# One-hots of four tiles made by two 512-wide VectorE instructions instead of four 128-wide ones, in a two-layer graph network

## The reference, cut to what matters

```python
# layer 0
m    = relu(concat(h[src], edge_attr) @ W_msg.T + b_msg)
m    = relu(m @ W_msg2.T + b_msg2)
mean = segment_sum(m, dst) / maximum(count(dst), 1)
x    = x + concat(h, mean) @ W_apply.T + b_apply
# layer 1, on h = relu(layernorm(x))
alpha = softmax of edge_weight over the edges of each destination
agg   = normalise(segment_sum(alpha * h[src], dst))
comb  = normalise(0.5 * (h @ W_self + b_self + agg @ W_nb + b_nb))
x     = x + layernorm(comb) * gamma + beta
```

## Time and profile before

| what | us |
|---|---|
| median of three runs | 8538.44 |
| the profiled execution | 8539.41 |
| its span, first to last instruction | 8537.0 |
| POOL busy | 6174.3 (72%) |
| PE busy | 5259.4 (62%) |
| VectorE busy | 3575.8 (42%) |
| ScalarE busy | 1110.0 (13%) |

### The profile page before, as it was taken

How to read it: one execution, slowest core, us unless ns; L and a number is a source line. 1 busy time by engine, 2 the same in 40 slices (tenths; PEclk the granted TensorE clock), 3 DMA queues, 4 the chain that set the end, 5 groups by cost and what they waited for, 6 DMA issues and landing times.

```text
span 8537.0 us, 114672 instructions
## 1 busy us (share of the span) xinstructions
PE 5259.4 (62%) x26549; PEld 4057.1 (48%) x26549; DVE 3575.8 (42%) x13889; ACT 1110.0 (13%) x1838; POOL 6174.3 (72%) x6510
## 2 busy tenths in 40 slices
PE   4887888888878888887844444444444444444444
PEld 3555655566556665665634334333333333333333
DVE  6344444333443443443454343333333333333336
ACT  2222222222222222222210000000000000000001
POOL 2777777777777777777657777777777777777773
PEclk9988989898898989888865555555555555555555
DMA  5322222222222222233332222111111111111112
GB/s 159 96 79 77 79 75 80 78 79 79 78 78 80 79 79 80 79 87 104 84 95 66 66 65 64 54 53 53 53 53 53 53 53 53 53 53 53 53 53 71
DMA packets 393173, 613.42 MB, mean 72 GB/s; under 512 B 171379, under 2 KB 248927, under 8 KB 392223
## 3 DMA queue, kind: packets, MB, share of 16 engines
q0 software_dynamic: 206336, 422.99, 18.3%
q1 hardware_dynamic: 186784, 189.85, 8.0%
HBM read 576.45 MB, written 35.92 MB: 72 GB/s over the span
## 4 chain that ended last, share of the span: by engine, by line
POOL 61%; issue 23%; PE 8%; DMA 4%; DVE 3%; POOLq 1%; SPq 1%; DVEq 0%; ACT 0%; ACTq 0%
POOL rows_ring L449 61%; PE bank L907 3%; DMA rows_ring<-p_table,idx 2%; PE bank L969 2%; DMA idx<-in_src_ring 1%; PE bank L966 1%; PE bank L904 1%; PE bank L1031 1%; POOLq L443 0%; DVE xq L629 0%; DVE acc L629 0%; POOLq L445 0%; DVE acc L614 0%; DVE stat L597 0%; DVE acc L717 0%
## 5 line engine op out<-in xcount | busy, mean ns | idle before, releaser
L449 POOL DMA_INDIRECT rows_ring<-p_table,idx x3224 | 3070.8, 952 | 1149.0 <-issue 1094.3
L780 DVE TENSOR_TENSOR acc<-acc,bank 128x128 f32 x6448 | 1829.3, 284 | 4826.0 <-PE bank L907 4813.9
L449 POOL DMA_INDIRECT rows_ring<-h_table,idx x3224 | 3050.6, 946 | 1025.7 <-issue 982.2
L907 PE MATMUL bank<-onehot,rows_ring 128*128 128x128 f32 x6448 | 1646.5, 436 | 2322.5 <-DMA rows_ring<-h_table,idx 2322.1
L907 PEld LDWEIGHTS bank<-onehot,rows_ring 128*128 128x128 f32 x6448 | 1415.5, 323 | 2553.4 <-issue 2363.9
L783 DVE TENSOR_SCALAR onehot<-iota,dloc,coef 128x128 f32<-128x128 f32 x6448 | 2340.8, 368 | 20.7 <-ACT coef L503 18.7
L907 PEld LDWEIGHTS bank<-wmat,work 128*128 128x128 f32 x7248 | 1104.0, 219 | 48.9 <-DVE acc L848 9.4
L907 PE MATMUL bank<-wmat,work 128*128 128x128 f32 x7248 | 1100.9, 303 | 11.6 <-DVE acc L848 10.0
L969 PE MATMUL bank<-work,we_sb 64*128 64x512 f32 x1612 | 987.4, 695 | 0.0
L907 PE MATMUL bank<-onehot,work 128*128 128x128 f32 x6448 | 945.3, 295 | 3.0 <-DVE onehot L783 2.9
L966 PE MATMUL bank<-ident,rows_ring 128*128 128x128 f32 x3224 | 546.6, 295 | 628.8 <-DMA rows_ring<-p_table,idx 624.0
(11 more groups left out here) (118 smaller groups left out, 837.9 us busy)
## 6 DMA issues: line engine op xcount, KB each, us to landing
work<-in_edge_t SPq DMA_DIRECT2D x403, 256.0 KB
rows_ring<-p_table,idx POOLq DMA_INDIRECT x3224
rows_ring<-h_table,idx POOLq DMA_INDIRECT x3224, 2.5
idx<-in_src_ring SPq DMA_DIRECT2D x404, 8.0 KB, 1.6
ht_rows<-rows_ring SPq DMA_DIRECT2D x25, 256.0 KB, 2.4
p_table<-rows_ring SPq DMA_DIRECT2D x25, 256.0 KB, 2.5
work<-ht_rows SPq DMA_DIRECT2D x25, 256.0 KB, 2.6
h_table<-work SPq DMA_DIRECT2D x25, 256.0 KB, 2.3
```

Source lines behind the costliest of these rows:

```text
L449: pool.indirect_dma_start(out=rows_ring[:, 16 * h + G * k + j, :], out_offset=None, in_=table[:, :], in_offset=bass.IndirectOffsetOnAxis(a ...
L780: dve.tensor_tensor(win, win, ps_agg[k % 2][:, j * P:(j + 1) * P], ALU.add).then_inc(added, 1)
L907: ins = pe.matmul(tiles(dst)[t], left[t], right[t] if isinstance(right, list) else right, start=bias is None and n == 0, stop=n == len(pai ...
```

## The change

The four `tensor_scalar` instructions of a group are replaced by two `tensor_tensor` instructions over all four tiles: first a comparison of `iota`, repeated four times, with `dloc` broadcast along each tile's 128 columns, and then, in place, a multiplication by `coef`, broadcast in the same way. The comparison stands ahead of the four adds and the multiplication behind them. A new semaphore `hot_compared` orders the second behind the first, and an increment of a counter stands between the wait and the multiplication.

```diff
-            def sums_and_onehots(i, k, lag_sum, lag_hot, in_psum, added, hot):
+            def sums_and_onehots(layer, i, k, lag_sum, lag_hot, in_psum, added, hot):
 
                 adds, hots = live(i, k, lag_sum), live(i, k, lag_hot)
                 gs, gh = 8 * i + k - lag_sum, 8 * i + k - lag_hot
                 if adds:
                     at = bases(gs)
                     dve.wait_ge(in_psum, gs + 1)
-                for j in range(G):
-                    if adds:
-                        if later(gs * G + j):
-                            dve.wait_ge(added, gs * G + j)
-                        win = acc[:, ds(at[j], P)]
-                        dve.tensor_tensor(win, win, ps_agg[k % 2][:, j * P:(j + 1) * P], ALU.add).then_inc(added, 1)
-                    if hots:
-                        t = gh * G + j
-                        ins = dve.tensor_scalar(onehot[:, k % 2, j * P:(j + 1) * P], iota[:, :], dloc[:, ds(t, 1)], coef[:, ds(t, 1)],
-                                                ALU.is_equal, ALU.mult)
                 if hots:
-                    ins.then_inc(hot, 1)
+                    hot4 = four(onehot[:, k % 2, :])
+                    dloc4, coef4 = (arr[:, ds(gh * G, G)].unsqueeze(2).to_broadcast([P, G, P]) for arr in (dloc, coef))
+                    dve.tensor_tensor(hot4, iota[:, :].unsqueeze(1).to_broadcast([P, G, P]), dloc4, ALU.is_equal).then_inc(S["hot_compared"], 1)
+                for j in range(G) if adds else ():
+                    if later(gs * G + j):
+                        dve.wait_ge(added, gs * G + j)
+                    win = acc[:, ds(at[j], P)]
+                    dve.tensor_tensor(win, win, ps_agg[k % 2][:, j * P:(j + 1) * P], ALU.add).then_inc(added, 1)
+                if hots:
+                    dve.wait_ge(S["hot_compared"], layer * NG + gh + 1)
+                    dve.sem_inc(S["vector_turns"], 1)
+                    dve.tensor_tensor(hot4, hot4, coef4, ALU.mult).then_inc(hot, 1)
```

More of the change, by code:

```diff
@@ L166, in gnn @@
             scalars_staged scalars_turned coef_filled sums_zeroed0 dloc_ready x_reloaded
-            counts_made m1t_in_psum m1t_ready m2_in_psum m2_ready onehot0_ready sums0_in_psum sums0_added
+            counts_made m1t_in_psum m1t_ready m2_in_psum m2_ready hot_compared onehot0_ready sums0_in_psum sums0_added
             x1_sums_copied x1_in_psum x1_added var1_ready root1_ready normed1_ready h2_ready sums_zeroed1
@@ L774, in sums_and_onehots @@
                     dve.wait_ge(in_psum, gs + 1)
-                for j in range(G):
-                    if adds:
-                        if later(gs * G + j):
-                            dve.wait_ge(added, gs * G + j)
-                        win = acc[:, ds(at[j], P)]
-                        dve.tensor_tensor(win, win, ps_agg[k % 2][:, j * P:(j + 1) * P], ALU.add).then_inc(added, 1)
-                    if hots:
-                        t = gh * G + j
-                        ins = dve.tensor_scalar(onehot[:, k % 2, j * P:(j + 1) * P], iota[:, :], dloc[:, ds(t, 1)], coef[:, ds(t, 1)],
-                                                ALU.is_equal, ALU.mult)
-                if hots:
-                    ins.then_inc(hot, 1)
+                if hots:
+                    hot4 = four(onehot[:, k % 2, :])
[10 more added lines that the diff above has]
+                    dve.tensor_tensor(hot4, hot4, coef4, ALU.mult).then_inc(hot, 1)
             def layer0(i):
                 for k in range(8):
-                    sums_and_onehots(i, k, 2, 0, S["sums0_in_psum"], S["sums0_added"], S["onehot0_ready"])
+                    sums_and_onehots(0, i, k, 2, 0, S["sums0_in_psum"], S["sums0_added"], S["onehot0_ready"])
             dve.wait_ge(S["coef_filled"], FILLS)
@@ L821, in layer1 @@
                 for k in range(8):
-                    sums_and_onehots(i, k, 2, 0, S["sums1_in_psum"], S["sums1_added"], S["onehot1_ready"])
+                    sums_and_onehots(1, i, k, 2, 0, S["sums1_in_psum"], S["sums1_added"], S["onehot1_ready"])
             dve.wait_ge(S["coef_filled"], 2 * FILLS)
```

## The result

The changed kernel takes 8972.24 us (median of four runs, 8970.26 to 8985.37) against 8538.97 us of the kernel before (8536.38 to 8539.82): a ratio of 1.0511, 95% interval 1.0498 to 1.0525. It is slower by 433 us; the forecast was 9023 us.

A forecast was written before the change was run, and what follows sets the result against it. The prediction took POOL issuing gathers back to back as the bound. To 8539.4 us it added 339 for layer 1 and 161 for layer 0, less 15 for removed one-hots: 9023 us against the median, range 8740 to 9208.

The forecast's parts named there:

- What bounds the kernel: POOL issuing 6,448 gathers back to back, 1.25 us apart: 8060 us, nearly the whole 8537 us span.
- VectorE: Per group, two 0.69 us instructions replace four 0.34 us one-hots: busy time unchanged, longer chain hidden in slack, costing nothing.
- S: Moment TensorE releases VectorE for a group; comparison forecast from it to 0.69 us later, multiplication from about 2.07 us later.
- The mark: 0.12 us after a gather's start; a VectorE instruction with two SBUF inputs running then holds the gather to its end.
- rival B: Faster: two inputs, one broadcast, do not stop POOL's gathers, so only 15 us are won: 8523 us; chance 0.06.
- Layer 1: Comparison hits one gather in each of 806 groups for 0.42 us, multiplication none: 339 us, bounds 81 and 403.
- f: Time from VectorE's release to the start of a gather beside it; in layer 1 claimed locked, 0.19 and 0.06 us shown.
- Rival A2: Layer 1's comparison starts 0.1 later and mostly misses: 0.15 us a group, 121 us instead of 339, 8805 us; chance 0.20.
- A: The forecast case: each comparison in layer 1 hits a gather, 9023 us; chance 0.65.
- Layer 0: Gather starts wander against VectorE's new instructions, so both together delay 0.20 us a group: 161 us, bounds 81 and 282.
- What was removed: Delays of gathers by the old one-hots, which go with the change: 15 us won, bounds 8 and 33.
- The sum: Profiled 8539.4 us plus 339 and 161 minus 15 gives 9024, or 9023 against the median.

The follow-up runs named there:

- e10: Changed kernel with comparison reading the constant row from PSUM and writing to PSUM, multiplication reading that: 8527.08 us in one run, kernel before 8546.43.
- e4: Changed kernel with only the multiplication losing its second SBUF input, the comparison writing to PSUM: 10889.93 us on a slower chip, kernel before 10992.57.
- e5: Changed kernel with only the comparison losing its second SBUF input, constant row read from PSUM: 10988.61 us on a slower chip, kernel before 10992.57.
- c1: The changed kernel unaltered, run again beside the kernel before: 8933.69 us against 8546.43, ratio 1.0456.

## Why the prediction was right, point by point

**What bounds the kernel.** Right, and it still does: the span grew by 431.5 us and the gathers by 432, with "issue" unchanged to 1.1 us.

**VectorE.** The new instructions take 697 and 694 ns where 0.69 was taken from the add of beta. The multiplication starts at S+2.15 in most groups; 2.07 plus up to 0.2 was forecast. The longer chain costs nothing where gathers are the bound: e10 has it whole and takes 8527.08 us.

**The mark.** A gather ends 0.81 to 0.83 us behind the instruction that holds it, as the three rows of before said. That the cause is the second SBUF input, which those rows could only suggest, is shown by e10, with e4 and e5. What the prediction had only as a guess is the other edge, "about 0.05" behind the start of the instruction. For the new instructions it is sharp: gathers that start up to 0.043 us behind one are let through, those that start 0.044 us or more behind it are held. For the old one-hots it is another, about 0.12 us. The clause of the Trainium skill ("SBUF — State Buffer", "Who interferes with whom") by which `tensor_tensor` would leave DMA issue alone does not hold for these indirect gathers; the same section's sentence that two SBUF inputs contend with a GpSimd instruction that reads SBUF fits, if an indirect gather counts as one. No run here separated its reading of the indices from the rest of its work. A broadcast input, rival B's doubt, makes no difference.

**Layer 1, the term that was mis-sized.** Forecast 339 us (0.42 in each of 806 groups), measured 239.6 + 47.3 + 5.1 = 292 us. The step that failed is "the comparison hits one gather in each group" and that f stays locked. f was locked only within the jitter of the landings, and 169 of 803 groups had f below 0.04 (the gather may start up to 0.1 us before the comparison among them). There the comparison lets the gather through (6013.58), and the multiplication catches the second one behind it, for 0.26 us (6016.08). The prediction saw this case and priced it at 0.1 to 0.15; it costs more because the multiplication starts at S+2.15 and not at S+2.07, and because f is about zero or less. That delay falls between the group's last gather and the next ones and so is added to f: 158 of those 169 groups are followed by one with f between 0.2 and 0.5, whose comparison then costs only 0.28 us (6018.83). Rival A2 was thus no alternative to A but a fifth of its groups, and dearer than its 0.15 a group, with 0.26 + 0.28 in two groups. Two groups that are hit were put at 0.44 + 0.44; the 403 with f from 0.044 to 0.2 measure 0.48 each.

**Layer 0.** Forecast 161 us, measured 66.8 + 90.8 = 158 us. Near because f is spread, where the average over the phase is a fair estimate.

**What was removed.** Forecast 15 us, measured 6.1 + 8.1 = 14 us. It is so small because of the edge at 0.12 us: 1,650 gathers had their mark inside a one-hot, but only 320 of them were held, for at most 0.34 - 0.12 - 0.12 = 0.10 us (the longest takes 1038 ns). In e10, where nothing takes their place, the one run is 8546.4 - 8527.1 = 19 us shorter than the kernel before.

**The sum.** The forecast growth was 339 + 161 - 15 = 485 us, the measured one 432; 47 of the 53 us between them are layer 1's term.

## What to carry to other kernels

If GpSimd issues indirect gathers back to back, a VectorE instruction with two SBUF inputs that runs over the beginning of one can hold it for most of its own length (here up to 0.53 us of 0.69), though VectorE has time to spare and the instruction counts fall. Four short `tensor_scalar` instructions were better here than two long `tensor_tensor` instructions of the same total length: they cost POOL 14 us where the new ones cost some 444 us. They differ in length and in kind, and the kind has its part, since a one-hot lets through what starts within 0.12 us of it; four short instructions with two SBUF inputs were not run. If a wide `tensor_tensor` is wanted, let one operand come from PSUM; then look at the gathers' mean in the trace, not at VectorE's busy time.

## What the runs showed of the hardware that was not expected

- The hold works the other way too: a comparison that starts 0.01 us before a gather lets it through and takes 0.74 us in place of 0.69. In the whole trace 165 of the new instructions start 0 to 0.043 us before a gather, and they take 723 to 767 ns where undisturbed ones take 692. In e10 such comparisons take 699 ns like all others.
- Eight two-input instructions without a wait held one gather for 4.31 us in the kernel before, and let three in, at 1.16 to 1.26 us, in the changed one. So rows 8 show what can happen, and not what always does.
- A fixed phase between engines turns a small shift into a large one. Between the trace of the first set of runs and c1's the same kernel lost 292 and 176.9 + 77.3 + 4.0 = 258 us in layer 1, by the groups with f below the edge.
- Chips differ far more than the change does: the same kernel takes 8.54 to 8.55 ms in two sets of runs and 10.98 to 11.24 ms in the four on other chips, with sequencer instructions of up to 1398 ns and up to 1.9 ms of waiting for indices, and there the version of e10 is 1.2 to 1.4% slower than the kernel before.
